# Two pieces of VectorE work in front of S4's sum, and another order of splits and small matmuls in the prologue

## The reference, cut to what matters

```
x = x + ffn0(cond0(x))      # cond0: x W0^T + 2 * top-2-gated LoRA (8 experts, rank 16, language bias on the router)
                            # ffn0: top-1-gated LoRA of cond0's output only
x = x + ffn1(cond1(x))      # cond1: x W1^T + b1 + 2 * LoRA slot picked per sequence (rank 16)
                            # ffn1: x Wb^T + b_base + 2 * top-2-gated LoRA (8 experts, rank 16)
out = x                     # 8 sequences x 256 rows x 1024
```

## Time and profile before

| | |
|---|---|
| median of 3 runs | 483.11 us |
| the profiled execution | 482.63 us |
| its span | 480.6 us |
| granted TensorE clock | 1.0 of full speed |
| TensorE / VectorE / ScalarE / GpSimd busy | 97% / 68% / 32% / 15% |
| DMA, mean | 84 GB/s |

### The profile page before, as it was taken

How to read it: one execution, slowest core, us unless ns; L and a number is a source line. 1 busy time by engine, 2 the same in 40 slices (tenths; PEclk the granted TensorE clock), 3 DMA queues, 4 the chain that set the end, 5 groups by cost and what they waited for, 6 DMA issues and landing times.

```text
span 480.6 us, 8350 instructions
## 1 busy us (share of the span) xinstructions
PE 465.5 (97%) x2911; PEld 429.5 (89%) x2911; DVE 328.0 (68%) x956; ACT 154.3 (32%) x340; POOL 72.9 (15%) x64
## 2 busy tenths in 40 slices
PE   6998999999999999999999999999999999999997
PEld 5987899999999898889899899999999999989996
DVE  3857765585675798849749848856865975973842
ACT  4565430232312354224223313323423322421320
POOL 2021000000000432222120240240221222210010
PEclk9999999999999999999999999999999999999999
DMA  8993448311112101221421421440340342110202
GB/s 263 384 324 133 125 137 156 122 44 45 44 45 63 31 20 27 27 44 62 96 46 61 96 46 30 111 59 16 111 61 11 105 59 37 61 51 2 73 33 87
DMA packets 88689, 40.25 MB, mean 84 GB/s; under 512 B 68647, under 2 KB 82737, under 8 KB 88526
## 3 DMA queue, kind: packets, MB, share of 16 engines
q1 hardware_dynamic: 88558, 39.81, 31.6%
q0 software_dynamic: 96, 0.00, 0.3%
HBM read 28.64 MB, written 11.16 MB: 83 GB/s over the span
## 4 chain that ended last, share of the span: by engine, by line
PE 85%; DVE 9%; issue 3%; ACT 2%; DMA 1%; SPq 0%; DVEq 0%; ACTq 0%
PE banks L1411 25%; PE banks L1413 25%; PE banks L1412 25%; PE banks L1427 4%; PE banks L1406 3%; DVE ybuf L1122 2%; PE banks L1662 2%; DVE G L928 2%; DVE left L928 1%; PE banks L1463 1%; DMA routers<-in_L_ffn_route_w_dram 1%; ACT left L668 1%; PE banks L1667 0%; PE banks L1436 0%; PE banks L1570 0%
## 5 line engine op out<-in xcount | busy, mean ns | idle before, releaser
L1411 PE MATMUL banks<-G,left 128*128 128x460 f32 x224 | 88.0, 393 | 0.0
L1413 PE MATMUL banks<-G,left 128*128 128x460 f32 x224 | 82.9, 370 | 0.0
L1412 PE MATMUL banks<-G,left 128*128 128x460 f32 x224 | 82.9, 370 | 0.0
L608 POOL TENSOR_TENSOR xTlo<-x_raw,xThi 128x512 fp32r<-128x512 f32 x28 | 38.4, 1393 | 249.5 <-ACT xThi L668 116.4
L1411 PE MATMUL banks<-WbThi,ws_hi 128*128 128x460 f32 (+1 forms) x216 | 75.1, 348 | 0.0
L1413 PE MATMUL banks<-WbThi,ws_lo 128*128 128x460 f32 (+1 forms) x216 | 73.3, 340 | 0.0
L1412 PE MATMUL banks<-WbTlo,ws_hi 128*128 128x460 f32 (+1 forms) x216 | 73.1, 338 | 0.0
L668 ACT ACTIVATE left<-x_raw 128x512 fp32r<-128x512 f32 x64 | 38.7, 628 | 60.0 <-DVE x_raw L1091 29.3
L1411 PEld LDWEIGHTS banks<-G,left 128*128 128x128 f32 x224 | 42.9, 191 | 4.5 <-DVE wzTlo L928 0.3
L1413 PEld LDWEIGHTS banks<-G,left 128*128 128x128 f32 x224 | 42.1, 188 | 4.7
L1412 PEld LDWEIGHTS banks<-G,left 128*128 128x128 f32 x224 | 42.3, 189 | 2.6
(11 more groups left out here) (213 smaller groups left out, 1002.2 us busy)
## 6 DMA issues: line engine op xcount, KB each, us to landing
x_raw<-in_x_dram SPq DMA_DIRECT2D x56, 128.0 KB, 3.7
out_dram<-ybuf SPq DMA_DIRECT2D x14, 512.0 KB, 2.7
x_raw<-in_L_cond_W_dram SPq DMA_DIRECT2D x10, 512.0 KB, 6.7
wraw<-in_L_cond_W_dram SPq DMA_DIRECT2D x5, 512.0 KB, 7.0
wraw<-in_L_ffn_W_base_dram SPq DMA_DIRECT2D x4, 512.0 KB, 10.0
x_raw<-in_L_ffn_W_base_dram SPq DMA_DIRECT2D x4, 512.0 KB, 8.4
a0f<-in_L_ffn_A_dram SPq DMA_DIRECT2D x2, 512.0 KB, 9.0
xin_first<-in_x_dram SPq DMA_DIRECT2D x1, 1024.0 KB, 14.8
```

Source lines behind the costliest of these rows:

```text
L608: return gp.tensor_tensor(out_, a, b, ALU.subtract)
L1411: pe.matmul(out_, l[0], r[0], start=start, stop=False, **kw)
L1412: pe.matmul(out_, l[0], r[1], start=False, stop=False, **kw)
L1413: return pe.matmul(out_, l[1], r[0], start=False, stop=stop, **kw)
```

## The change

1. In every block VectorE does hs_part(m + 1) and top1(a) in front of S4's sum, not behind it.
2. C0's last two row blocks are done by halves: both for k = 0 to 3 (then `c0_done`), then both for k = 4 to 7.
3. D0's 8 steps are cut in 5 and 3; the a0 units are turned between the parts. ScalarE and VectorE take the a0 units in front of D0's result.
4. TensorE waits for all low parts up to q = 16 behind the turn of q = 17, not in front of it. ScalarE takes q = 17's hi part in front of exp0, and VectorE its low part inside gates0, where it would wait for exp0.
5. ScalarE and VectorE take five units (18 to 22) in front of hgT_part(0) and two (23, 24) behind; before, it was four (17 to 20) in front and four (21 to 24) behind.

```diff
 # ScalarE
             xT_part(0, 0, xT_first, XT_FIRST[0])
+            copy_units(3, units_a0)
             act.wait_ge(d0w_done, 1)
             act.activation(D0hi[:, :], p0[:, 0:RC], ACT.Copy, scale=2.0).then_inc(d0w_hi, 1)
-            copy_units(3, units_a0)
...
             copy_units(NU1, units_second[:NEF - NU1])
+            copy_units(NEF, units_second[NEF - NU1:NEF - NU1 + 1])
             exp0(0)
-            copy_units(NEF, units_second[NEF - NU1:NEF - NU1 + 4])
+            copy_units(NEF + 1, units_second[NEF - NU1 + 1:NEF - NU1 + 6])
             hgT_part(0)
-            copy_units(NEF + 4, units_second[NEF - NU1 + 4:NEF - NU1 + 8])
+            copy_units(NEF + 6, units_second[NEF - NU1 + 6:NEF - NU1 + 8])
             keep_fe(0)
 # VectorE: the same in lo_units, and
-            gates0(0, 0)
-            lo_units(NEF, units_second[NEF - NU1:NEF - NU1 + 4])
+            gates0(0, 0, lambda: lo_units(NEF, units_second[NEF - NU1:NEF - NU1 + 1]))
+            lo_units(NEF + 1, units_second[NEF - NU1 + 1:NEF - NU1 + 6])
...
+                hs_part(m + 1, 1)
+                if has_a:
+                    top1(a)
                 s_sums(b, turn, (3,))
-                hs_part(m + 1, 1)
-                if has_a:
-                    top1(a)
                 if b == 0:
                     lo_last((T2, T4))
 # TensorE
-            for j in range(K):
+            for j in range(K - 2):
...
+            for half in range(2):
+                for j in (K - 2, K - 1):
+                    pe.wait_ge(w0_lo, j + 2)
+                    for k in range(half * KH, half * KH + KH):
+                        ins = c0_step(j, k)
+                    if half == 1:
+                        ins.then_inc(w0_used, 1)
+                    elif j == K - 1:
                         ins.then_inc(c0_done, 1)
...
             pe.wait_ge(b0_lo, 1)
-            for j in range(K):
-                ins = three(p0[:, 0:RC], ...)
-            ins.then_inc(d0w_done, 1)
+            d0_steps(0, 5)
             pe.wait_ge(c0_sum, 2)
             turn_units(3, units_a0)
+            d0_steps(5, K)
...
-            pe.wait_ge(unit_lo, NEF)
             for n, unit in enumerate(units_second[NEF - NU1:NEF - NU1 + 10]):
...
                 turn_units(NEF + n, [unit])
+                if n == 0:
+                    pe.wait_ge(unit_lo, NEF)
```

More of the change, by code:

```diff
@@ L981, in _ @@
             xT_part(0, 0, xT_first, XT_FIRST[0])
+            lo_units(3, units_a0)
             dve.wait_ge(d0w_hi, 1)
             lo(D0lo[:, :], p0[:, 0:RC], D0hi[:, :], 2.0).then_inc(d0w_lo, 1)
-            lo_units(3, units_a0)
             G_STEPS = 8
@@ L1187, in _ @@
             dve.tensor_copy(bcol[:, :], pt[:, 0:K]).then_inc(bcol_ready, 1)
-            gates0(0, 0)
-            lo_units(NEF, units_second[NEF - NU1:NEF - NU1 + 4])
+            gates0(0, 0, lambda: lo_units(NEF, units_second[NEF - NU1:NEF - NU1 + 1]))
+            lo_units(NEF + 1, units_second[NEF - NU1 + 1:NEF - NU1 + 6])
             hgT_part(0)
-            lo_units(NEF + 4, units_second[NEF - NU1 + 4:NEF - NU1 + 8])
+            lo_units(NEF + 6, units_second[NEF - NU1 + 6:NEF - NU1 + 8])
             keep_fe(0)
@@ L1336, in slot @@
                     y_c22(b - 1)
-                s_sums(b, turn, (3,))
                 hs_part(m + 1, 1)
@@ L1340, in slot @@
                     top1(a)
+                s_sums(b, turn, (3,))
                 if b == 0:
@@ L1417, in _, with c0_step @@
             turn_units(0, units_r0)
-            for j in range(K):
+            def c0_step(j, k):
+                for n, w in enumerate(split_of(w0s_hi[j % 4], w0s_lo[j % 4], k)):
+                    ins = pe.matmul(banks[:, k, 0:2 * RC], w, R0T[:, j, :], start=j == 0 and n == 0,
+                                    stop=j == K - 1 and n == 1)
+                return ins
+            for j in range(K - 2):
                 pe.wait_ge(unit_lo, j // 3 + 1)
@@ L1425, in _ @@
                         pe.wait_ge(unit_lo, 3)
[L1426 to L1429, removed]
+                    ins = c0_step(j, k)
[4 more added lines that the diff above has]
+                    for k in range(half * KH, half * KH + KH):
+                        ins = c0_step(j, k)
+                    if half == 1:
+                        ins.then_inc(w0_used, 1)
+                    elif j == K - 1:
                         ins.then_inc(c0_done, 1)
-                ins.then_inc(w0_used, 1)
             def turn_x(src, at):
@@ L1442, in _, with d0_steps @@
             turn_x(xin_first[:, 0:D], XT_FIRST[0])
+            def d0_steps(j0, j1):
+                for j in range(j0, j1):
+                    ins = three(p0[:, 0:RC], split_of(b0hi, b0lo, j), (R0Thi[:, j, :], R0Tlo[:, j, :]),
+                                j == 0, j == K - 1)
+                    if j == K - 1:
+                        ins.then_inc(d0w_done, 1)
             pe.wait_ge(b0_lo, 1)
-            for j in range(K):
-                ins = three(p0[:, 0:RC], split_of(b0hi, b0lo, j), (R0Thi[:, j, :], R0Tlo[:, j, :]),
-                            j == 0, j == K - 1)
-            ins.then_inc(d0w_done, 1)
+            d0_steps(0, 5)
             pe.wait_ge(c0_sum, 2)
             turn_units(3, units_a0)
+            d0_steps(5, K)
             def small0(t, left, step=None):
```

## The result

| | before | after |
|---|---|---|
| median of 6 runs each | 483.09 us | 478.81 us |
| lowest, highest | 482.14, 483.39 | 477.66, 481.05 |
| the profiled execution, its span | 482.63, 480.6 | 481.05, 478.9 |
| ratio, 95% interval | | 0.9914 [0.9894, 0.9934] |

What follows compares the result with a forecast made beforehand. TensorE, busy 97% of the span, was taken as the bound. 482.63 - 2.1 (prologue) - 3.6 (blocks) = 476.9, with the median 0.48 above: 477.4 us; own range 476.5 to 478.3, widened up to 479.6.

Steps and rivals of the forecast that it cites:

- (a): Rival: the prologue's gain is caught by VectorE at units 20 to 24 or a late load; 478.7 us, 15%.
- (b): Rival: in the blocks GpSimd blocks top1, wh becomes late as hs was; blocks give half, 1.8 us: 479.2; 12%.
- Part 1: Prologue, C0's last rows by halves: the x turn on TensorE starts 0.6 us earlier.
- Part 2: Prologue, D0 in two parts: small0 1.05 us earlier, of which 0.75 remain at unit 9.
- Part 3: Prologue, unit 17's turn put into the 1.26 us wait: gain 0.4, to 1.2 us in all.
- Part 4: Prologue, five units in front of hgT_part: unit 24's turn 2.1 us earlier, at 48.9.
- Does it last?: Step: from 57 to 165 us TensorE is never idle, so the prologue's whole 2.1 us comes through.
- Part 5: Blocks, S4's sum behind hs_part and top1: waits for hs and wh go, 3.6 us; bounds 0 and 3.6.
- rival (c): S4's sum comes too late for ScalarE, lost in seven blocks; 1 us late would give 484.4; 4%.
- The last block: Step: in the last block nothing waits for hs, so the blocks' new order changes 0 there.
- The signs: If right: x turn 26.4, unit 24 near 48.9, no earlier idle over 0.2, blocks' distance 1.53, sum 0.68 in each.

Runs made afterwards that it cites:

- e5: The kernel after with C0's last rows done in one go again; 477.71 us, one execution.
- e6: The kernel after with D0 whole again, its copies in front of the a0 units'; 478.96 us, one execution.
- e8: The kernel after with the wait for low parts and unit 17 back in their old places; 478.28 us, one execution.
- e3: The kernel after with S4's sum in front of hs_part again in the last block alone; 477.34 us, ratio 0.9886.
- e11: The kernel after, unchanged, run once more; 478.33 us.
- e4: The kernel before with only GpSimd changed: its xT low parts wait for S4's sum; 486.43 us, ratio 1.0081.
- e2: The kernel after with the blocks' old order, so the prologue edits alone; 481.37 us, ratio 0.9973.
- e9: The kernel after with the top choice behind S4's sum again, only hs_part in front; 480.18 us, ratio 0.9944.
- e10: e3 with GpSimd's prologue copy from a0c to b_j waiting until hg is made; 477.27 us, ratio 0.9883.
- e12: e3 unchanged, run again beside e10 and e11; 477.26 us.

## Why the prediction was right, and where it was off

The direction and both large terms (1.9 for 2.1, 3.55 for 3.6) came as reckoned. The number is less good: 478.81 lies outside the forecast's own range of 476.5 to 478.3, and inside the wide one up to 479.6, which was stretched for rivals (a) and (b). Neither of them happened; what filled that room was something else, and that it fitted is luck.

- **Part 1** was forecast at 0.6; 0.63 in the profile, and 0.64 by undoing it (e5).
- **Part 2**: small0 1.05 earlier, unit 9 0.75. Measured 0.99 and 0.67. What I had not separated: with D0 whole (e6) unit 9 comes at the same time. All that passes unit 9 is part 1's; the split alone is worth nothing there.
- **Part 3**: 0.4 more at the first fe product, 1.2 in all. Measured 0.42 (e8) and 1.08.
- **Part 4**: unit 24 2.1 us earlier. Measured 1.90 without the collision, with unit 21's turn held as the text said, and 1.4 to 1.5 with it (27.97 - 26.60 in e3, 27.97 - 26.45 in e11, at the second x turn). Here the size was off: I took VectorE's way from the choice to hg as free of GpSimd, as it had been in the one profile that I had, and the change itself moves it onto GpSimd's copy.
- **Does it last?** It did: 1.10 us of difference at the second x turn, 1.07 at hg's turn in block 0, and from 60 to 168 us TensorE of the kernel after is busy 108.0 of 108.0, as in the earlier trace rows. Rival (a) fell.
- **Part 5**: 3.6 us, 0.82 for block 1 and 0.52 to 0.66 for the others. Measured 3.55, every distance at 1.52 or 1.53, line 1119 at 0.68 in these seven blocks. Block 0 changed nothing, as reckoned. TensorE waited for none of what S4's part on ScalarE and the loads feed; rival (c) fell.
- **The last block** is the step of the prediction that failed: "In the last block nothing waits for hs: 0". True of hs, but the sum was moved there too, and I looked only at who waits for hs, not at what the sum would meet in its new place. It met GpSimd's low part of S3, and pushed the gates onto the next one. Measured +0.75.
- **Rival (b)** did not happen in the kernel after, but my reason against it was wrong. That the first hs part keeps its time beside GpSimd says nothing of the top choice: its input is in PSUM, that of the top choice's CAST in SBUF. e4 shows the rival at work, six waits of 1.0 us. So it was right about the kernel after by 0.35 us of room in block 1, which was not reckoned, and not by its reason. The profile of before even had a short instruction held: a 128x128 SCALAR_TENSOR_TENSOR with both inputs in SBUF (Mdir, at 160.79) took 0.83 us for 0.28, with GpSimd at work from 160.18 to 162.78.
- **The signs.** No wait at the hs turn and a distance of 1.53 came true. "No idle bracket before it over 0.2" did not: 0.46 stands in front of unit 9, 0.68 in front of the first fe product and 0.69 in front of unit 21, and the last two are in the prediction's own Part 3. A new bracket stands at the line of wh's turn too, but it is wz's, in the last block. Line 1119 is at 0.68 in seven blocks and at 1.42 in the last.

From 477.4 to 478.8: 0.75 for the last block, 0.2 to 0.7 for the prologue. The rest, up to 0.5, would lie in the start, by what is left over and not by a measurement of its own: the runs of the kernel after spread over 3.4 us and the profile shows one with C0 3.0 us late. e2's profile has C0's last product at 28.73, e2's twelve runs spread over 2.9 us; in all the other profiles it starts between 25.6 and 27.1. Both late ones have the whole new prologue; e3, e9, e10, e11 and e12 have it too and started on time, as did e5 to e8 with one part of it undone, and the late load is issued ahead of every changed instruction. The kernel before has an outlier too, 485.07 us, 2.1 above the median of the nine runs beside e9 to e12, with no profile to say why. Whether the change makes late starts more frequent is left open; no run here varied the loads.

The Trainium skill, "SBUF — State Buffer", section "Who interferes with whom", says that the shared ports are an exclusive lock, that casts and tensor_scalar can take it in their two-port modes, when their operands meet the conditions for them, and that the order of issue decides who blocks. The traces agree in what they can show, the durations, and not which mode was taken: CAST 0.73 for 0.17, TENSOR_SCALAR 1.20 for 0.29, and the add that takes 0.17 when it starts 0.03 us ahead of GpSimd and 1.26 when it starts 0.05 behind. I cited the section for the sum alone, and dismissed casts because the profile of before showed none stretched; that profile has only one from SBUF that overlapped (at 460.18), with the last 0.11 us of a GpSimd instruction, where nothing can be seen.

## What to carry to other kernels

Before you move an instruction, list what the other user of the SBUF ports does at its new place in every iteration, the first and the last too, where the schedule differs; then list which instructions it pushes onto something. A short instruction on the way to TensorE, if it is of a kind that is held, is worth as much care as a long one: here a 128x8 add that takes 0.17 us waited 1.1 us for the end of GpSimd's instruction. In this kernel leaving one iteration in the old order was worth 1.07 us of the 5.7 that the best version gains. And measure landmarks from a common event (here C0's last product) before comparing two profiles, or the landing of a load, and the pace of TensorE behind it, pass for an effect of the change.

## What the runs showed of the hardware

- VectorE beside a GpSimd instruction that reads SBUF: held to its end were TENSOR_TENSOR with both inputs in SBUF (128x512, 0.68 to 1.42 us; 128x8, 0.17 to 1.26), SCALAR_TENSOR_TENSOR with both inputs in SBUF (128x128, 0.28 to 0.83), CAST from SBUF (128x2, 0.17 to 0.73) and TENSOR_SCALAR (128x8, 0.29 to 1.20). MAX8 (0.17), FIND_INDEX8 (0.16), COPY and CAST out of PSUM (0.16 and 0.19), a 128x1 RECIPROCAL (0.16), a 128x1 TENSOR_SCALAR (0.14) and SCALAR_TENSOR_TENSOR with one input in PSUM (0.17, 0.29) kept their times beside it, so some of the kernel's VectorE work overlaps GpSimd for free.
- GpSimd can lose as well: its xT low part in block 0 took 3.37 us with the sum beside its first half (before) and 2.92 with the sum behind it (after). In block 1, where the sum lay beside the second half, it took 2.83 in both.
- The loads of W0's second rows landed up to 1.7 us apart in the profiles of before and after (ScalarE's copy at 9.52 and 11.25), and over all profiles C0's last product started between 25.6 and 29.3.
- Behind a wait of 2.0 us the granted TensorE clock of the kernel after stood at 0.52 (the 1.2 GHz level) from 14.3 to 17.6 us, and matmuls of 272 columns started 0.226 us apart and not 0.126. In e2, behind a wait of 0.73 us, 17 of them had the same slow pace at a granted clock of 1.00; what set it there is open.
